# First attention of a four-layer transformer kernel: stacked rows of two batches by a selection matrix on TensorE, and the loads in another order

## The chip, the cores and the metric

One core of a Trainium2 chip runs the whole program in one launch. The metric is the device time of that launch in microseconds (us). The kernel before took 1108.44 us (median of three runs).

## What is computed

The reference is four layers, each `x = x + attention(layernorm(x))` and `x = x + ffn(layernorm(x))`, with another attention and another feed-forward block in each layer. Only the first attention is changed. For `x` and `ctx` of shape (8, 128, 512) and a mask of shape (8, 1, 512), it works on 32 patches of 128 columns (4 of each of 8 batches):

```python
q = einsum('ed,bdw->bew', Wq, x_patch) + bq        # 64 rows = 8 heads x 8
k = einsum('ed,bdw->bew', Wk, x_patch) + bk
val = einsum('ed,bdw->bew', Wv, ctx_patch) + bv
scores = einsum('bhdi,bhdj->bhij', qh, kh) / sqrt(8)
scores = where(mask > 0, scores, -1e9)
o = einsum('bhij,bhdj->bhdi', softmax(scores), vh)
out = (einsum('de,bew->bdw', Wo, gelu(o)) + bo) * mask
```

## The kernel before

The first attention is the function `l0_attention` (line 284). Each engine has its own program, written out by hand; the engines meet only at semaphores, and each runs its instructions strictly in the order written. The layers stand one behind the other with a barrier between them (`end_layer`, line 70), so the stage ends for all engines at once.

**Batches and units.** The eight batches `b` are worked through in order. A batch is two units `u` (`A0_GROUPS`, four heads each), a unit is two steps `s` (two heads each). For a batch, VectorE (DVE) takes the statistics of `x[b]` (line 100 and 102), GpSimd (POOL) makes 1/sigma of them (lines 106 and 109), DVE (b < 3) or POOL (b >= 3) normalises (lines 597, 496), and TensorE (PE) projects queries and keys together (`project`, line 694). DVE adds the bias and multiplies by `kept`, which DVE (b = 0) or POOL makes of the loaded mask (lines 608, 360). The result `qk` is split into an fp32r upper part (ScalarE, ACT, line 541) and a rest (line 653 on DVE for b = 0, line 484 on POOL for the others).

**The stacked rows.** A score matmul needs, at the partitions of its head, 26 rows: the 8 rows of the upper part twice, the rest once, a row for the maximum and a row for the mask. The kernel before gets them through DRAM: `store(b)` (lines 409 to 418) writes the parts in five DMAs to `a0_parts`, and `fetch(b)` (lines 420 to 428) reads them back in four DMAs into the stack `st`, in the order wanted. The constant rows of all batches are written once (lines 437 to 441).

**The loop over the units.** Scores (line 723), their maximum on DVE (line 628), the maximum turned on PE (line 732), added to the queries on DVE (`lower`, line 638), scores again with that subtracted (`keyed`, line 742), exponent on ACT (line 557), values (line 753), a copy and a turn (lines 564, 760), and a division on DVE. In iteration u, PE runs:

```python
turn_max(u); scores(2u+2); keyed(2u-1)
project(batch_at(u))         # u odd: batch (u + 5) // 2, so 3 at u=1, 4 at u=3 ... 7 at u=9
project_values(...)          # u even
values(u-1); scores(2u+3); keyed(2u); turn_outputs(u-1)
```

DVE runs `divide(u-2)`, `maximum(2u+2)`, `statistics(statistics_at(u))`, `keys_queries(batch_at(u))`, `lower(u)`, `maximum(2u+3)`. `statistics_at(u)` (line 383) gives batch u // 2 + 4 at even u, and batch 3 stands ahead of the loop (line 662). POOL runs, for each batch from 3 on, `first.scale(b)` (waits for the statistics), `keep_rows(b)` (waits for the mask's load), `normalise(b)`, `lower_part(b)`, lines 525 to 529.

**The queue of SyncE (SP)**, which issues all loads and stores of the stage, is in a fixed order (lines 430 to 470), with waits between; what stands behind a wait is issued after it. Here the mask of batch 3 is loaded (line 453) ahead of `store(2)` and behind `fetch(1)`.

## Time and profile before

| | |
|---|---|
| runs | 1108.44 us median, 1107.95 to 1110.77 (3 runs) |
| the profiled execution | 1100.67 us, its span 1098.9 us |
| mean granted clock of TensorE in it | 0.926 |
| busy, share of the span | PE 86%, DVE 62%, ACT 41%, POOL 34% |
| first attention | 0 to 165.6 us of the span |
| first score matmul | 28.35 us |
| first turn of a maximum (unit 0) | 34.52 us |
| DMAs up to 130 us | 21.83 MB, mean 168 GB/s |

The span is the profiled execution alone, seen from the first to the last instruction; 1.8 us of its time lie around it. In the views, L694 is line 694 of the kernel before. SPq marks the issue of a DMA, not its transfer. A TensorE row with x2 or x8 is a run of that many instructions, with the time from the first start to the last end; an fp32 matmul shows as two instructions.

### The profile page before, as it was taken

Reading aid. Unit: us, or ns where it says so; the run is one execution under the profiler, and the core shown is the slowest. Engines: PE = TensorE matmul, PEld = TensorE weight load, DVE = VectorE, ACT = ScalarE, POOL = GpSimd, SP = SyncE. Lnnn points to the kernel's source line nnn. Section 1 sums busy time; section 2 is a strip of 40 time slices with the busy share of each in tenths; the row PEclk is TensorE's granted clock in tenths of the full one; section 3 lists DMA queues with packets and bytes.
Section 4 is the critical chain, followed back from the end, with each engine's and each line's share of the span. In section 5 each row is a group of like instructions: output and inputs, shape, how many; then the busy total and the mean of one; then the engine's idle time right before and its main releaser. Section 6 shows DMA issues by size and latency. Waiting matters only on the chain. (4 is left out here: it accounts for less than half of the span.)

```text
span 1098.9 us, 14895 instructions
## 1 busy us (share of the span) xinstructions
PE 941.0 (86%) x4891; PEld 610.1 (56%) x4891; DVE 683.1 (62%) x1143; ACT 447.4 (41%) x656; POOL 374.4 (34%) x362
## 2 busy tenths in 40 slices
PE   2788786989999899999877598899986689679997
PEld 0566623756666566663445344455473455457886
DVE  2566464686687687764858753566644887445334
ACT  0255413325656566652234422344403555235130
POOL 5552021224566565651222220211220222048431
PEclk9999855999999999999889699799988999879999
DMA  6766103146977967556304100000003100032001
GB/s 158 230 169 175 63 0 140 39 164 243 342 266 269 372 202 267 201 177 216 115 23 160 39 0 1 20 1 1 1 0 153 49 0 1 5 92 77 29 10 38
DMA packets 41237, 124.00 MB, mean 113 GB/s; under 512 B 5313, under 2 KB 5761, under 8 KB 38473
## 3 DMA queue, kind: packets, MB, share of 16 engines
q1 hardware_dynamic: 33640, 98.41, 26.7%
q0 software_dynamic: 7520, 24.65, 6.8%
q8 instruction: 40, 0.66, 0.3%
q14 instruction: 37, 0.30, 0.1%
HBM read 137.19 MB, written 23.59 MB: 146 GB/s over the span
## 5 line engine op out<-in xcount | busy, mean ns | idle before, releaser
L1275 POOL DMA_INDIRECT f_picks<-f_turn_xn,f_target x47 | 106.7, 2271 | 78.9 <-ACT f_turn_xn L1164 78.0
L1691 PE MATMUL banks<-f_t_dn,f_z 128*128 128x512 f32 x188 | 88.5, 593 | 0.6 <-issue 0.6
L1419 DVE TENSOR_TENSOR f_gu_lo<-f_t_gu,f_gu_hi 128x2048 fp32r<-128x2048 f32 x24 | 55.1, 2296 | 18.1 <-ACT f_gu_hi L1150 15.2
L1269 POOL DMA_INDIRECT f_turn_xn<-f_xn_rows,f_token x47 | 48.5, 1033 | 46.0 <-DVE f_token L1413 18.7
L1419 DVE TENSOR_TENSOR f_xn_lo<-f_t_gu,f_xn_hi 128x2048 fp32r<-128x2048 f32 x23 | 52.8, 2297 | 17.5 <-ACT f_xn_hi L1150 17.5
L628 DVE TENSOR_REDUCE a_mx<-banks 128x8 f32<-128x1024 f32 x32 | 39.2, 1226 | 27.1 <-PE banks L723 27.1
L2389 ACT ACTIVATE a_e<-banks 128x1024 f32<-128x1024 f32 x32 | 32.8, 1025 | 54.1 <-PE banks L2481 54.1
L2419 DVE TENSOR_REDUCE a_mx<-banks 128x8 f32<-128x1024 f32 x32 | 39.1, 1223 | 21.8 <-PE banks L2461 21.8
L1150 ACT CAST f_gu_hi<-f_t_gu 128x2048 fp32r x24 | 45.7, 1904 | 13.4 <-DMA f_t_gu<-in_f_gu 11.2
L1150 ACT CAST f_xn_hi<-f_t_gu 128x2048 fp32r x23 | 43.8, 1903 | 13.3 <-DMA f_t_gu<-in_f_gu 9.9
L1157 ACT ACTIVATE f_sil<-banks 128x256 f32<-128x256 f32 x47 | 18.1, 384 | 75.9 <-PE banks L255 75.9
L164 PE MATMUL banks<-ident,f_turn_xn 128*128 128x128 f32 x96 | 21.7, 382 | 31.4 <-DVE f_turn_xn L172 31.4
L100 DVE BATCH_NORM_STATS2 stat<-x_res 128x6 f32<-128x512 f32 x64 | 44.4, 693 | 3.5 <-DMA x_res<-in_x 1.6
L557 ACT ACTIVATE a_e<-banks 128x1024 f32<-128x1024 f32 x32 | 32.8, 1024 | 30.3 <-PE banks L742 29.9
L1691 PEld LDWEIGHTS banks<-f_t_dn,f_z 128*128 128x128 f32 x188 | 32.1, 190 | 23.3 <-issue 23.2
L253 PE MATMUL banks<-f_gu_hi,f_xn_hi 128*128 128x512 f32 x96 | 40.0, 416 | 2.1 <-issue 2.1
L106 POOL TENSOR_TENSOR f_ahead_var_eps<-mean_var,eps 128x1 f32<-128x1 f32 x24 | 9.0, 376 | 91.6 <-DVE mean_var L102 91.6
L253 PE MATMUL banks<-f_xn_hi 128*128 128x512 f32 x92 | 38.0, 413 | 1.3 <-issue 1.3
L3154 DVE TENSOR_TENSOR f_square<-f_relu 128x512 f32<-128x512 f32 x16 | 19.5, 1224 | 30.9 <-ACT f_relu L3097 25.9
L255 PE MATMUL banks<-f_gu_hi,f_xn_lo 128*128 128x512 f32 x96 | 38.0, 396 | 0.0
L254 PE MATMUL banks<-f_gu_lo,f_xn_hi 128*128 128x512 f32 x96 | 38.0, 396 | 0.0
L164 PEld LDWEIGHTS banks<-ident,f_turn_xn 128*128 128x128 f32 x96 | 15.4, 193 | 39.7 <-DVE f_turn_xn L172 39.4
(414 smaller groups left out, 2567.6 us busy)
## 6 DMA issues: line engine op xcount, KB each, us to landing
f_t_gu<-in_f_gu SPq DMA_DIRECT2D x47, 1024.0 KB
f_t_dn<-in_f_dn SPq DMA_DIRECT2D x47, 512.0 KB
f_t_gu<-f_picks SPq DMA_DIRECT2D x8, 1024.0 KB, 5.2
a_st<-a_parts SPq DMA_DIRECT2D x32, 208.0 KB
f_xn_rows<-f_turn_xn SPq DMA_DIRECT2D x9, 256.0 KB, 2.1
x_res<-in_x SPq DMA_DIRECT2D x8, 256.0 KB, 5.6
a_out_mask<-in_mask SPq DMA_DIRECT2D x8, 256.0 KB, 6.1
a_parts<-a_qk_hi SPq DMA_DIRECT2D x8, 256.0 KB
```

Of the source, the lines that this page charges most:

```text
L100: dve.bn_stats(self.stat[:, b, :], src).then_inc(self.stat_ready, 1)
L164: mm = pe.transpose(self.core.psum[:, self.first_bank + b % 2, c * P:(c + 1) * P], self.xn[:, b % self.rows, c * P:(c + 1) * P], self.core ...
L253: pe.matmul(out, w_hi, m_hi, start=start, stop=False)
L254: pe.matmul(out, w_hi, m_lo, start=False, stop=False)
L255: return pe.matmul(out, w_lo, m_hi, start=False, stop=stop)
L628: dve.tensor_reduce(mx[:, :, PAIR * (s % 2) + A0_MAX_ROW:PAIR * (s % 2 + 1):A0_SLOT].rearrange("p w r -> p r w"), ps[:, S_BANK:S_BANK + 2, ...
L1150: act.copy(t_gu_hi[t % 2], t_gu[:, bass.ds(i, 1), :, :].rearrange("p i c n -> p (i c n)"))\
L1269: pool.indirect_dma_start(t_rows[:, t % F0_BUFS, :], None, dram["f0_xn_rows"], bass.IndirectOffsetOnAxis(ap=token[:, t:t + 1], axis=0))\
L1275: pool.indirect_dma_start(dram["f0_picks_flat"], bass.IndirectOffsetOnAxis(ap=target[:, t:t + 1], axis=0), t_y[:, t % F0_BUFS, :], None).t ...
L1419: dve.tensor_tensor(t_gu_lo[t % 2], t_gu[:, bass.ds(i, 1), :, :].rearrange("p i c n -> p (i c n)"), t_gu_hi[t % 2].bitcast(F32), ALU.subtr ...
L1691: mm = pe.matmul(ps[:, TY_BANK + t % 2, :], t_zt[:, t % 2, c, :], t_dn[:, t % F0_BUFS, c, :], start=c == 0, stop=c == F0_IC - 1)
L2419: dve.tensor_reduce(mx[:, tiles, A2_MAX_ROW:P:A2_SLOT].rearrange("p m r -> p r m"), ps[:, S_BANK:S_BANK + 2, :].rearrange("p r (m j) -> p ...
```

## The change

Of batches 0 and 1 (`A0_DIRECT = 2`) the rows no longer go through DRAM. A selection matrix is drawn on chip out of the identity: VectorE clears a scratch of 128x1024, ScalarE copies four patterns of the identity into it and casts it to fp32r (128x1024), and a second small block of constant rows is made in the same way. For each of units 0 to 3, `stack(u)` on TensorE then makes the 128 rows of queries and the 128 rows of keys in PSUM: three matmuls with one row of contraction for the constant rows, and four with the selection matrix, two of the upper part and two of the rest. ScalarE copies the queries out of PSUM into the stack (`keep_queries`), VectorE the keys (`keep_keys`). Units 0 and 1 are stacked ahead of the loop, 2 and 3 at the end of iteration 0; behind them, in iteration 0, now stand the projection of batch 2 and the values of batch 0, which stood ahead of the loop. The clearing of the stack on POOL goes. Batches 2 to 7 are stored and fetched as before. The order of the loads, of POOL's early work and of the statistics is another: `statistics_at(u)` gives batch u // 2 + 3 at even u > 0, with batch 3 at the end of iteration 0.

The diff, cut (scratch names and semaphores left out):

```diff
+            sel = st[:, A0_DIRECT, 0:2, :]
+            drawn, drawn_rows = e[:, 0, 0:2, :], e[0:1, 0, 2:4, :]
+            off_rows = qm[0:1, 0:A0_DIRECT, :]
...
+            def sel_bank(u, keys):
+                return ((6, 7), (2, 1), (2, 1), (0, 2))[u][keys]
...
             def statistics_at(u):
-                return u // 2 + A0_EARLY + 1 if u % 2 == 0 and u // 2 + A0_EARLY + 1 < B else None
+                return u // 2 + A0_EARLY if u % 2 == 0 and 0 < u and u // 2 + A0_EARLY < B else None
...
                     load_x(0)
                     sp.dma_start(core.raw[:, 0, 0:A0_FIRST[-1]], dram["a0_first"]).then_inc(first_loaded, 16)
+                    load_mask(0)
+                    sp.dma_start(mask_rows, dram["mask"][0:A0_DIRECT].unsqueeze(0)).then_inc(mask_rows_loaded, 16)
+                    load_x(1)
+                    load_mask(1)
+                    load_x(2)
                     sp.dma_start(off_row[:, :], dram["mask"]).then_inc(mask_row_loaded, 16)
-                    load_mask(0)
-                    load_x(1)
-                    load_x(2)
...
-                    store(0)
-                    sp.wait_ge(fixed_stored, 16 * 3)
-                    load_mask(1)
                     load_mask(2)
                     load_ctx(0)
-                    fetch(0)
                     load_x(3)
-                    store(1)
+                    sp.wait_ge(fixed_ready, 2)
...
+                    sp.wait_ge(fixed_stored, 16 * 3)
+                    load_ctx(1)
                     load_x(4)
-                    load_ctx(1)
-                    fetch(1)
+                    store(2)
                     load_mask(3)
-                    store(2)
                     load_x(5)
                     load_ctx(2)
                     fetch(2)
...
(POOL)
-                    clear(0)
+                    pool.memset(mx[:, :, :], 0.0).then_inc(mx_zeroed, 1)
+                    for i in range(2):
+                        pool.memset(fixed[:, i, :], float(i)).then_inc(fixed_ready, 1)
                     first.scale(pool, 0)
+                    for i in range(2):
+                        pool.memset(v[:, i, :, :, :], 0.0).then_inc(zeroed, 1)
+                    first.scale(pool, 1)
...
                     keep_rows(1)
-                    lower_part(1)
-                    clear(1)
-                    keep_rows(2)
-                    lower_part(2)
+                    first.scale(pool, 2)
...
+                    lower_part(1)
+                    keep_rows(2)
+                    lower_part(2)
...
(ACT)
+                    def keep_queries(u):
+                        act.wait_ge(sel_done, 2 * u + 1)
+                        act.copy(q_of(u, slice(0, P), slice(0, D)), ps[:, sel_bank(u, 0), :]).then_inc(st_q_ready, 1)
-                    for b in range(A0_EARLY):
-                        upper_part(b)
-                    take_values(0)
+                    upper_part(0)
+                    keep_queries(0)
+                    keep_queries(1)
+                    upper_part(1)
                     for u in range(UNITS + 1):
...
+                        if u == 0:
+                            keep_queries(2)
+                            keep_queries(3)
+                            upper_part(2)
+                            take_values(0)
...
(DVE)
+                    def keep_keys(u):
+                        dve.wait_ge(sel_done, 2 * u + 2)
+                        dve.tensor_copy(k_of(u, slice(0, P), slice(0, D)), ps[:, sel_bank(u, 1), :])\
+                           .then_inc(st_k_ready, 1)
...
                     normalise(1)
-                    keys_queries(1)
-                    normalise(2)
-                    keys_queries(2)
+                    keep_keys(0)
+                    keep_keys(1)
+                    statistics(2)
                     dve.wait_ge(mx_zeroed, 1)
                     maximum(0)
+                    keys_queries(1)
                     maximum(1)
-                    statistics(A0_EARLY)
+                    normalise(2)
...
+                        if u == 0:
+                            keep_keys(2)
+                            keep_keys(3)
+                            keys_queries(2)
+                            statistics(A0_EARLY)
...
(PE)
+                    def stack(u):
...
+                        pe.matmul(queries, row_of(A0_MASK_ROW), ones_row, start=True, stop=False)
+                        pe.matmul(keys, row_of(A0_MAX_ROW), ones_row, start=True, stop=False)
+                        pe.matmul(keys, row_of(A0_MASK_ROW), off_rows[:, b, :], start=False, stop=False)
+                        pe.wait_ge(qk_hi_ready, b + 1)
+                        pe.matmul(queries, sel[:, 0, jobs[0]], hi, start=False, stop=False)
+                        pe.matmul(keys, sel[:, 0, jobs[1]], hi, start=False, stop=False)
+                        pe.wait_ge(qk_lo_ready, b + 1)
+                        pe.matmul(queries, sel[:, 1, jobs[0]], lo, start=False, stop=True).then_inc(sel_done, 1)
+                        pe.matmul(keys, sel[:, 1, jobs[1]], lo, start=False, stop=True).then_inc(sel_done, 1)
...
-                    for b in range(A0_EARLY):
-                        project(b)
-                    project_values(0)
-                    pe.wait_ge(const_ready, 4)
+                    project(0)
+                    stack(0)
+                    stack(1)
+                    project(1)
                     scores(0)
                     scores(1)
...
+                        if u == 0:
+                            stack(2)
+                            stack(3)
+                            pe.wait_ge(st_q_ready, 2 * A0_GROUPS)
+                            pe.wait_ge(st_k_ready, 2 * A0_GROUPS)
+                            project(2)
+                            project_values(0)
```

`stack(3)` waits ahead of its first matmul for the queries of unit 2 to be copied out of bank 2 (`st_q_ready` 3).

## Rows read from the trace of the kernel before

**Rows 1.** timeline 0 to 29 us: start, us, engine, line, operation, idle before it

```profile
6.38 2.04 PE L694 MATMUL banks<-a_xn,raw 128*128 128x512 f32 x2 [6.38 <-DVE a_xn L597]
...
16.84 1.41 SPq L399 DMA_DIRECT2D a_out_mask<-in_mask  x2
...
21.37 2.01 POOL L360 TENSOR_SCALAR a_kept<-a_out_mask,a_cols 128x512 f32<-128x512 f32 x1 [9.11 <-DMA a_out_mask<-in_mask]
...
23.49 0.75 DVE L608 SCALAR_TENSOR_TENSOR a_qk<-banks,a_cols,a_kept 128x512 f32<-128x512 f32 x1 [11.63 <-POOL a_kept L360]
...
27.37 0.57 SPq L418 DMA_DIRECT2D a_parts<-a_qk_lo  x1
...
28.35 1.11 PE L723 MATMUL banks<-a_st 26*128 26x128 f32 x8
```

**Rows 2.** timeline 34 to 45 us, all engines

```profile
34.52 1.11 PE L732 MATMUL banks<-ident,a_mx 128*128 128x128 f32 x4 [1.32 <-DVE a_mx L628]
...
34.72 0.37 SPq L399 DMA_DIRECT2D a_out_mask<-in_mask  x1
...
39.40 1.11 PE L742 MATMUL banks<-a_qm,a_st 26*128 26x128 f32 x8 [0.19 <-DVE a_qm L638]
...
40.55 2.00 POOL L360 TENSOR_SCALAR a_kept<-a_out_mask,a_cols 128x512 f32<-128x512 f32 x1 [3.18 <-DMA a_out_mask<-in_mask]
...
42.54 2.09 POOL L496 TENSOR_SCALAR a_xn<-x_res,mean_var,rstd 128x512 f32<-128x512 f32 x1
...
44.68 2.08 PE L694 MATMUL banks<-a_xn,raw 128*128 128x512 f32 x2 [1.85 <-POOL a_xn L496]
```

**Rows 3.** timeline 52 to 94 us, projections of batches 4 to 7, statistics before them

```profile
53.42 0.18 DVE L102 BATCH_NORM_AGGREGATE mean_var<-stat 128x2 f32<-128x6 f32 x1
...
58.39 2.07 PE L694 MATMUL banks<-a_xn,raw 128*128 128x512 f32 x2 [1.39 <-POOL a_xn L496]
...
61.96 0.33 PE L723 MATMUL banks<-a_st 26*128 26x128 f32 x2
...
67.10 0.18 DVE L102 BATCH_NORM_AGGREGATE mean_var<-stat 128x2 f32<-128x6 f32 x1
...
70.60 1.13 PE L694 MATMUL banks<-a_xn,raw 128*128 128x512 f32 x2
...
72.87 0.55 PE L723 MATMUL banks<-a_st 26*128 26x128 f32 x6
...
81.51 1.13 PE L694 MATMUL banks<-a_xn,raw 128*128 128x512 f32 x2
...
93.15 1.12 PE L694 MATMUL banks<-a_xn,raw 128*128 128x512 f32 x2 [0.66 <-POOL a_xn L496]
```

**Rows 4.** timeline of TensorE at 186 us, a dense stretch of fp32r matmuls

```profile
186.65 0.63 PE L254 MATMUL banks<-f_xn_lo,f_gate_hi 128*16 128x512 f32 x1
...
187.08 0.63 PE L255 MATMUL banks<-f_xn_hi,f_gate_lo 128*16 128x512 f32 x1
...
188.38 0.39 PE L253 MATMUL banks<-f_xn_hi,f_gate_hi 128*16 128x512 f32 x1
...
188.60 0.40 PE L254 MATMUL banks<-f_xn_lo,f_gate_hi 128*16 128x512 f32 x1
```

**Rows 5.** groups by line and form, VectorE, whole span

```profile
L2148 DVE CAST a_q_st<-banks 128x512 fp32r<-128x512 f32 x16 | 11.0, 687 | 7.4 <-PE banks L2251 7.4
```

**Rows 6.** DMA issues up to 130 us: size, us from issue to landing

```profile
raw<-in_a_first SPq DMA_DIRECT2D x1, 98.0 KB, 2.5
```

**Rows 7.** timeline at 10 us: 1/sigma of batch 1 on POOL

```profile
10.11 0.19 POOL L106 TENSOR_TENSOR in_ahead_var_eps<-mean_var,eps 128x1 f32<-128x1 f32 x1 [0.72 <-DVE mean_var L102]
...
10.38 0.57 POOL L109 TENSOR_TENSOR rstd<-in_ahead_var_eps,neg_half 128x1 f32<-128x1 f32 x1
```

**Rows 8.** windows: stretch, length, busy us of PE, PEld, DVE, ACT, POOL, clock, DMA share, GB/s

```profile
58.00:60.00 2.00, 1.61 (x2) 0.50 (x2) 0.24 (x1) 0.13 (x1) 0.33 (x1) 0.54 0.84 209
...
116.00:118.00 2.00, 1.99 (x36) 1.60 (x40) 0.67 (x2) 0.13 (x1) 0.00 (x0) 0.55 0.00 0
```

99 lines of the change are left out of this document (72 added, 27 removed).

## The prediction

> **What bounds the kernel now.** I read the page for the shares, then the timeline of the first 60 us, the waits in it, the timelines of VectorE, POOL, TensorE and of SP's queue up to 165 us, and the windows for the clock. The stage of the change ends in a barrier, so what its end gains or loses goes to the total whole. The start is bound by the way through DRAM: batch 0 is projected at 6.38, and its first score matmul comes at 28.35 [rows 1]. Between them lie the store, the fetch, and the mask of batch 1, which is issued behind the store at 16.84 and releases POOL only at 21.37. The first maximum is turned at 34.52 [rows 2]. From there the units run at their own pace, and something else binds: PE works in order, and in every odd unit stands a projection of a later batch ahead of the work of the unit. In unit 1 PE waits for POOL's normalised batch 3 until 44.68, after POOL has waited for the mask of that batch (issued 34.72, used 40.55) [rows 2]. In unit 3 it waits again (1.39 us, project at 58.39). In units 5 and 7 (70.60 and 81.51) it waits for nothing, in unit 9 for 0.66 us [rows 3]. So the question is not how early unit 0 starts, but when batch 3 can be projected, and whether batches 4 to 7 are ready when PE gets there.
>
> **The early start.** Removed are store(0), store(1), fetch(0), fetch(1) and three clears of the stack, added are 28 matmuls, eight copies out of PSUM and the drawing of the matrix. The drawing ends well ahead of the first use at about 10 us: it is a clear and a few copies while x is loaded, and where it ran over, PE would wait for it by that much; I put it at nothing, with 1 us as the upper end. project(0) ends at 8.4. The 14 matmuls of stacks 0 and 1 are fp32r with 512 columns. The trace has such a stream at both levels of the clock: 0.43 us from start to start at 1.2 GHz (186.65 to 187.08), 0.22 at 2.4 GHz (188.38 to 188.60), with the granted clock at one half and at one [rows 4]. At the start PE is at the lower level by its durations (2.04 for a projection [rows 1] against 1.13 at 70.60 [rows 3]). So 14 x 0.43 = 6.0 and 0.2 for the wait for the parts: 14.6, then project(1) to 16.7, and the scores of step 0 there. Up to keyed(0) follow one behind the other four scores and the turn, 1.11 each [rows 2], and three maxima of 1.2: 9.2, so keyed(0) at about 25.9 against 39.40 [rows 2]. A dense stretch of 6 us stands ahead of this, though, and in the trace such a stretch brought the clock up [rows 4]. At the upper level for part of the way (stack 1, project(1) and the scores of step 0) keyed(0) is at 23.7, and at the upper level all the way at about 22. I take 23.7, which lies between. The lead over before is then 15.7 us.
>
> **Where the lead goes.** keyed(0) ends at 24.8. Stack 2 and stack 3 come then, and stack 3 waits for the copy of unit 2's queries: 7 x 0.43 = 3.0, 0.3 for the end of the last matmul and 0.69 for a copy [rows 5]; stack 3 can start behind the copy of the queries, one matmul ahead of the stack's end, at 28.2. Its keys are copied at 32.2 by the same sum, and at 30.6 with the clock at its upper level by then; I take 31.5. Only then may project(2) write its bank: 1.13 to 2.04, so 32.7. Before, from qk in VectorE to the end of the last issue of its store took 23.49 to 27.94, 4.45 us [rows 1]. SP comes to the mask of batch 3 only behind `store(2)`: 37.2, where it was issued at 34.72 before. The order of these two is turned round, and that is the step that costs. **The load** of this mask is priced by the mask of batch 1, which stood behind a store too: 16.84 to 21.37, 4.5 us. Its ends are 2.5 us (a load of 98 KB with little ahead of it [rows 6]) and 5.8 us (34.72 to 40.55, with a fetch ahead). 4.5 is the nearest, as its queue is the same. So POOL begins at 41.7, and needs 2.00 for kept and 2.09 for the normalised batch (40.55 to 44.68: 4.1): **project(3) at 45.9 against 44.68, 1.2 us later than before.** All the lead is spent in PE's wait in unit 1. With PE at the lower level all the way, keyed(0) is at 25.9, project(2) ends at 36.2 and project(3) starts at 49.3: 4.6 later. At the upper level all the way from stack 1, project(2) ends at 28.3, and project(3) starts at 41.4: 3.3 earlier.
>
> The Trainium skill (DMA: Bandwidth & Descriptors, Anatomy of one DMA — SWDGE (gpsimd) path) has a fit of 2.0 us and the bytes over 436e3 per us, which makes 2.6 us for this mask's 256 KB instead of 4.5, and by it the sum below would be 1.9 less, 1115.1. The trace speaks against it for a mask behind a store.
>
> **The statistics.** They slip by one even unit. Batch 4's now stand in unit 2, batch 5's in 4, batch 6's in 6, batch 7's in 8, where before the batch after it stood. POOL works in order: 1/sigma (10.11 to 10.95, with a tenth ahead of it: 0.93 [rows 7]), kept 2.00, normalise 2.09, together 5.05 from the end of the statistics to the projection. Nothing hides this any more, as both the statistics and the use stand two units nearer.
> - Batch 4: statistics end at 53.60 + 5.05 = 58.65 against 58.39 [rows 3]: +0.3.
> - Batch 5: 67.28 + 5.05 = 72.35 against 70.60: +1.75.
> - Batch 6: the same, one period of 10.91 later (70.60 to 81.51): +1.75.
> - Batch 7: 67.28 + 21.82 + 5.05 = 94.15 against 93.15: +1.0.
>
> Together +4.8, each on top of the shift so far, since the statistics move with the unit.
>
> **The clock.** Before project(4) PE stood for 1.39 us, and the granted clock was 0.54 in the window behind it; in the window from 116 it was 0.55, behind a stretch of short waits with no projection [rows 8]. From such a projection to the next scores it took 3.57 (58.39 to 61.96) against 2.27 at the upper level (70.60 to 72.87) [rows 3]: 1.3 us for a fall. PE now stands 1.75 us at batches 5 and 6 and 1.66 at batch 7, longer than at batch 4, but at batch 7 with 0.66 before it did not fall. I take two falls of three, 2.6 us; the ends are 0 and 3.9.
>
> **At nothing**: the removed clears on POOL, whose idle time hides them; the traffic of two batches less through DRAM, as neither PE nor DVE waits for a fetch in any of the rows from 52 us on; the copies of stacks 2 and 3 on ACT and VectorE, which are in the sum already, and what lies in unit 1 between, which PE's wait for batch 3 covers. If that cover is gone (project(3) early), they count as in the sum of project(3).
>
> **Sum**: +1.2 +4.8 +2.6 = +8.6 us in this stage. Against the profiled execution (1098.9 span, 1100.67 with what lies around it) that is 1109.3; the median of the runs is 7.8 above the profiled one, and I add the same to it: 1108.4 + 8.6 = **1117.0 us**.
>
> **The rivals.**
> - *The clock stays up.* Stacks 0 and 1 bring PE to 2.4 GHz and it stays there. For it: a dense stretch of this kind rose to it in the trace. Against: in units 0 and 1 PE mostly waits for maxima, and before it was at the lower level there for all of 28 to 45 us. Then project(3) is 3.3 earlier, PE comes to batches 5 to 7 without a fall, and the fall at 58 may go too: -3.3 +4.8 -1.3 = +0.2, 1108.6, not slower. It decides from the point at which project(3) starts before 40 us. Chance 0.14.
> - *The clock stays down up to unit 1.* +4.6 +4.8 +3.9 = +13.3, 1121.7. Chance 0.18.
> - *No fall at batches 5 to 7.* +1.2 +4.8 = +6.0, 1114.4. Chance 0.20.
> - *The lead is kept*: the change does what it says for the total, since neither mask 3 nor the statistics hold PE. Unit 0 turned some 15 us earlier would give 1093. For it: SP may have less queued, and the mask land early. Against: the order of SP, PE and POOL is written out, and a mask issued at 37 can't feed a projection before 43. Chance 0.06.
>
> **The numbers.** The forecast as summed has 0.42. A measurement of this kernel can tell about 0.3%, 3.3 us, from no change. Slower by more: the forecast, the low clock, and most of the case without falls, with 0.02 to 0.03 off for its lower end: 0.75. Faster: the kept lead and a little of the first rival: 0.08. Within: 0.17. The range takes in the first rival's 1108.6 and the second's 1121.7: 1108.5 to 1122.
>
> **What would show it.** Scores of step 0 at 15 to 17 us, keyed(0) at 23 to 26. SP's issue of mask 3 at 36 to 41, behind the last piece of store(2). PE idle for 7 us or more ahead of project(3), released by POOL, at 44 to 49. The projections of batches 5 to 7 released by POOL with 1.6 us or more of idle time, where two of them had none, and project(7) at 95 to 102 against 93.15. Stage end at 170 to 178 against 165.6. The forecast is wrong if project(3) comes before 42, or if the idle time ahead of project(5) and project(6) is under 1 us; and it is wrong in its clock term if the granted clock stays at one behind them.

## The result, and the profile after

The changed kernel takes 1126.1 us (median of 4 runs, 1124.74 to 1128.23) against 1108.2 for the kernel before (4 runs, 1106.48 to 1110.77): a ratio of 1.0161, 95% interval 1.0135 to 1.0188. It is 17.9 us slower, where 8.6 were forecast; the direction was right, the size was not, and the time lies above the range. The profiled execution took 1128.23 us, with a span of 1126.4. One execution of the first experiment below (1127.89 us) fell in a slower state of the chip, at a lower granted clock, and is left out of its numbers.

The start of the changed kernel, from the timelines of VectorE and TensorE (start, duration, engine, line, tiles; in brackets the idle time ahead and what ended it; `...` marks rows left out):

```profile
5.39 2.04 DVE L636 TENSOR_SCALAR a_xn<-x_res,mean_var,rstd 128x512 f32<-128x512 f32 x1 [0.95 <-POOL rstd L109]
7.58 2.05 PE L750 MATMUL banks<-a_xn,raw 128*128 128x512 f32 x2 [7.58 <-DVE a_xn L636]
...
15.73 0.63 PE L799 MATMUL banks<-a_qk_lo,a_st 128*128 128x512 f32 x1
16.16 0.63 PE L800 MATMUL banks<-a_qk_lo,a_st 128*128 128x512 f32 x1
...
18.42 1.11 PE L813 MATMUL banks<-a_st 26*128 26x128 f32 x8
...
23.55 1.09 PE L822 MATMUL banks<-ident,a_mx 128*128 128x128 f32 x4 [1.41 <-DVE a_mx L667]
...
36.82 2.04 PE L750 MATMUL banks<-a_xn,raw 128*128 128x512 f32 x2 [0.83 <-ACT a_st L597]
```

The early start is there: the first scores come at 18.42 instead of 28.35 [rows 1], the first maximum is turned at 23.55 instead of 34.52 [rows 2]. But the stacks' matmuls are still 0.43 us apart at the end of stack 1 (15.73, 16.16), the distance of 1.2 GHz [rows 4], and the scores behind them take 1.11 for eight, as at the start of before. The signs that the forecast gave for this part are missed: 15 to 17 us for the first scores, and 23 to 26 for keyed(0), which starts at 27.60. Project(2) runs from 36.82 to 38.9, where 32.7 was forecast for its end.

The same view from project(2) to project(3), with SP's queue:

```profile
38.91 0.75 DVE L647 SCALAR_TENSOR_TENSOR a_qk<-banks,a_cols,a_kept 128x512 f32<-128x512 f32 x1 [2.18 <-PE banks L750]
...
42.93 0.57 SPq L433 DMA_DIRECT2D a_parts<-a_qk_lo  x1
43.55 0.46 SPq L414 DMA_DIRECT2D a_out_mask<-in_mask  x1
...
48.29 2.00 POOL L371 TENSOR_SCALAR a_kept<-a_out_mask,a_cols 128x512 f32<-128x512 f32 x1 [5.83 <-DMA a_out_mask<-in_mask]
...
52.41 2.08 PE L750 MATMUL banks<-a_xn,raw 128*128 128x512 f32 x2 [10.02 <-POOL a_xn L507]
```

This is the chain of the forecast link by link: the store's last piece, the mask behind it, POOL's two operations (the second from 50.27 to 52.35), and PE idle for 10.02 us. Only its start is late: mask 3 is issued at 43.55, where 36 to 41 was given, and project(3) starts at 52.41, outside 44 to 49.

TensorE's timeline of the later units: the projections of batches 4 to 7, most of the turns of the maxima (one a unit), the first output projection (L867), and on VectorE the first operation of the next stage:

```profile
58.72 1.12 PE L822 MATMUL banks<-ident,a_mx 128*128 128x128 f32 x4 [0.25 <-DVE a_mx L667]
67.04 1.12 PE L822 MATMUL banks<-ident,a_mx 128*128 128x128 f32 x4 [0.26 <-DVE a_mx L667]
69.16 2.07 PE L750 MATMUL banks<-a_xn,raw 128*128 128x512 f32 x2
74.57 0.66 PE L822 MATMUL banks<-ident,a_mx 128*128 128x128 f32 x4 [0.54 <-DVE a_mx L667]
80.02 0.66 PE L822 MATMUL banks<-ident,a_mx 128*128 128x128 f32 x4 [0.23 <-DVE a_mx L667]
82.94 2.08 PE L750 MATMUL banks<-a_xn,raw 128*128 128x512 f32 x2 [1.65 <-POOL a_xn L507]
...
89.25 1.11 PE L822 MATMUL banks<-ident,a_mx 128*128 128x128 f32 x4 [0.25 <-DVE a_mx L667]
...
99.68 2.07 PE L750 MATMUL banks<-a_xn,raw 128*128 128x512 f32 x2
...
105.19 0.66 PE L822 MATMUL banks<-ident,a_mx 128*128 128x128 f32 x4 [0.54 <-DVE a_mx L667]
...
113.56 2.08 PE L750 MATMUL banks<-a_xn,raw 128*128 128x512 f32 x2 [1.64 <-POOL a_xn L507]
...
173.91 1.38 PE L867 MATMUL banks<-a_gelu,a_wo 64*128 64x512 f32 x2
...
196.34 1.00 DVE L172 TENSOR_SCALAR f_turn_xn<-x_res,mean_var,rstd 128x512 f32<-128x512 f32 x2 [2.35 <-PEq L75]
```

Two kinds of unit can be seen. With turns of 0.66 us a unit takes 5.45 us (74.57 to 80.02), half of the 10.91 between two projections before [rows 3]; with turns of 1.12 it takes 8.3 us (58.72 to 67.04). PE is hardly idle in either. The projections start later than before by 7.7, 10.8, 12.3, 18.2 and 20.4 us, and the stage ends 30.7 later (196.34 against 165.63). PE waits for POOL at batches 5 and 7 (1.65 and 1.64, forecast 1.75 and 1.66), and not at all at batches 4 and 6, where 1.7 and 1.75 were forecast. The window from 60 to 120 us shows what PE did in the rest (busy time of PE, its loads, VectorE, ScalarE and POOL; then the granted clock, the share of the DMA engines, GB/s). First before, then after:

```profile
60.00:120.00 60.00, 51.13 (x819) 38.74 (x818) 41.09 (x60) 31.67 (x41) 19.48 (x16) 0.96 0.57 149
```
```profile
60.00:120.00 60.00, 53.71 (x613) 38.34 (x614) 33.84 (x51) 24.93 (x32) 24.39 (x20) 0.77 0.56 139
```

PE is busier than before and gets through 613 matmuls where it did 819. (The column of the clock says 1.00 up to the first change that the trace records, in after at 82 us; by the durations PE was low there up to some 72 us, so the 0.77 is still too high.)

From project(3) to project(7) it takes 61.2 us (52.41 to 113.56) instead of 48.5 (44.68 to 93.15), though the waits for POOL in it grow only from 2.05 to 3.29. The eight units between them at 5.45 make 43.6 in both. What is left is 2.8 before and 14.3 after. The turns tell how it is made up, before in these rows:

```profile
50.27 0.66 PE L732 MATMUL banks<-ident,a_mx 128*128 128x128 f32 x4 [0.54 <-DVE a_mx L628]
...
63.95 0.66 PE L732 MATMUL banks<-ident,a_mx 128*128 128x128 f32 x4 [0.54 <-DVE a_mx L628]
...
85.76 0.65 PE L732 MATMUL banks<-ident,a_mx 128*128 128x128 f32 x4 [0.38 <-DVE a_mx L628]
```

In both kernels PE comes out of some of its waits at the lower level. Before, this happens at batches 3 and 4, and both times it is up again at the next turn (0.66 at 50.27 and 63.95), at some 1.3 us each. After, it happens at batches 3 and 5, and both times it stays low over two turns and comes up only behind the next projection, ahead of which PE did not wait (69.16 and 99.68). From the projection to the third turn behind it such a spell takes 22.2 us (52.41 to 74.57, 82.94 to 105.19), where the same stretch at the upper level took 15.2 before (70.60 [rows 3] to 85.76): 7 us a spell, and two of them are the 14.3. So to come low out of a wait has two prices, 1.3 us or 7.

Behind project(7), with no wait for POOL left, PE is low again for most of the way: at the first output projection, 173.91 against 138.52 in the row of before that follows, the shift is 35.4 us instead of 20.4, which is 15 us more, as much as some five units at the lower level.

```profile
138.52 2.07 PE L777 MATMUL banks<-a_gelu,a_wo 64*128 64x512 f32 x2
```

From there to the end of the stage (196.34 against 165.63, 30.7 later) 4.7 us come back, since now it is before that is at the lower clock (2.07 for this operation, where after has 1.12 and 1.09 from its second batch on).

Of the 30.7 us, project(3) makes 7.7, the waits for POOL at the later batches 1.2, and the rest, 21.8 (11.5 + 15.0 - 4.7), goes by the units to the clock. In the stages behind, another 3.2 us come back (the spans differ by 27.5).

The profiled execution of before lies 7.5 under the median given here, that of after 2.1 over its own. So this pair differs by 27.6 us, the medians by 17.9: the two traces show the mechanism somewhat larger than it is on the whole.

### The profile page after: what moved, and what is told of

The parts are those of the page before. It is cut to its first block and busy times, and to the rows that moved or that the text cites. A ratio compares the mean times of both kernels' runs of the same rounds, so it can differ in the third digit from the quotient of the medians.

```text
span 1126.4 us, 14951 instructions
## 1 busy us (share of the span) xinstructions
PE 972.3 (86%) x4916; PEld 636.7 (57%) x4919; DVE 689.2 (61%) x1151; ACT 453.3 (40%) x666; POOL 375.7 (33%) x360
## 5 line engine op out<-in xcount | busy, mean ns | idle before, releaser
L1373 POOL DMA_INDIRECT f_picks<-f_turn_xn,f_target x47 | 114.6, 2439 | 73.8 <-ACT f_turn_xn L1262 73.4
L667 DVE TENSOR_REDUCE a_mx<-banks 128x8 f32<-128x1024 f32 x32 | 39.2, 1226 | 49.3 <-PE banks L813 49.3
L1517 DVE TENSOR_TENSOR f_gu_lo<-f_t_gu,f_gu_hi 128x2048 fp32r<-128x2048 f32 x24 | 55.1, 2294 | 15.8 <-ACT f_gu_hi L1248 13.9
L2517 DVE TENSOR_REDUCE a_mx<-banks 128x8 f32<-128x1024 f32 x32 | 39.1, 1223 | 21.8 <-PE banks L2559 21.8
```

What stands on the lines that cost most here:

```text
L667: dve.tensor_reduce(mx[:, :, PAIR * (s % 2) + A0_MAX_ROW:PAIR * (s % 2 + 1):A0_SLOT].rearrange("p w r -> p r w"), ps[:, S_BANK:S_BANK + 2, ...
L1373: pool.indirect_dma_start(dram["f0_picks_flat"], bass.IndirectOffsetOnAxis(ap=target[:, t:t + 1], axis=0), t_y[:, t % F0_BUFS, :], None).t ...
L1517: dve.tensor_tensor(t_gu_lo[t % 2], t_gu[:, bass.ds(i, 1), :, :].rearrange("p i c n -> p (i c n)"), t_gu_hi[t % 2].bitcast(F32), ALU.subtr ...
L2517: dve.tensor_reduce(mx[:, tiles, A2_MAX_ROW:P:A2_SLOT].rearrange("p m r -> p r m"), ps[:, S_BANK:S_BANK + 2, :].rearrange("p r (m j) -> p ...
```

## The experiments

The expectations name two theories. **W**: the waits for POOL, made longer by the later statistics and by the order of `store(2)` and mask 3, cost their own length, and the clock falls because of them, so that taking a wait away gives both back. **C**: the lower clock is entered and left by itself, whatever the wait, so that taking a wait away gives back its length alone. Each label below is one kernel; its ratio is to the kernel before on the same chip, with the 95% interval. Executions of all these kernels scatter more than the first runs had shown (25 of the kernel before gave 1100.47 to 1116.73 around 1107.75), so small differences are taken from ratios with intervals.

### The statistics back in their old place

```diff
-                return u // 2 + A0_EARLY if u % 2 == 0 and 0 < u and u // 2 + A0_EARLY < B else None
+                return u // 2 + A0_EARLY + 1 if u % 2 == 0 and 0 < u and u // 2 + A0_EARLY + 1 < B else None
...
                             statistics(A0_EARLY)
+                            statistics(A0_EARLY + 1)
```

> The changed kernel with the statistics back at their old even units (batches 3 and 4 at the end of iteration 0, 5 in unit 2, 6 in unit 4, 7 in unit 6); all else as changed. Changed kernel 1126.1 us. Theory W (the slipped statistics make PE wait for POOL ahead of the projections of batches 5 and 7, 1.65 and 1.64 us in the changed trace, and the clock falls because of these waits): both waits go, and with them the low clock behind them (82 to 102 us and 113 to 160 us), 3.3 us for the waits and 12 to 17 for the clock: 1106 to 1111 us. Theory C (TensorE's low clock is entered and left by itself, whatever the wait): only the waits go, about 1123 us.

Measured: 1110.8 us (9 runs, 1106.41 to 1119.89), ratio 1.0025 (0.9985 to 1.0065). That is 15.3 under the changed kernel (14.6 if the execution left out is counted), from a part for which the forecast had 4.8 in waits and 2.6 in clock. It is what W expected, and 12 us under what C did: much more comes back than the length of the waits. The profiled execution is the one left out, so nothing is rested on its trace.

### The mask ahead of the store

```diff
                     load_x(4)
-                    store(2)
                     load_mask(3)
+                    store(2)
```

> The changed kernel with the load of mask 3 issued ahead of store(2), one line moved. If the place of this load holds the projection of batch 3 (52.41 us in the changed trace), POOL starts on kept at 42.5, and project(3) at about 46.6, 5.8 us earlier: 1120 us. If what follows is set by the clock and not by the wait, the 5.8 us come back or are lost by other low stretches: anything from 1116 to 1126. If the load was no cause, 1126.

Measured: 1121.5 us (4 runs), ratio 1.0139 (1.0066 to 1.0213), 4.6 under the changed kernel. TensorE's timeline:

```profile
45.84 2.08 PE L750 MATMUL banks<-a_xn,raw 128*128 128x512 f32 x2 [4.18 <-POOL a_xn L507]
...
75.77 1.12 PE L750 MATMUL banks<-a_xn,raw 128*128 128x512 f32 x2 [1.63 <-POOL a_xn L507]
```

The start of project(3) and the time are as expected (46.6 and 1120 us). Project(3) is 6.6 us earlier than after (45.84 against 52.41), so the order of these two spent most of the lead, and from there on each projection stays ahead of its time in after. Project(5) runs at the upper level here (1.12) in spite of a wait of 1.63 us. For the total the step between medians, 4.6 us, points the same way, but the two intervals (1.0066 to 1.0213 and 1.0135 to 1.0188) lie over each other, so that its size is not secured.

### Both

```diff
-                return u // 2 + A0_EARLY if u % 2 == 0 and 0 < u and u // 2 + A0_EARLY < B else None
+                return u // 2 + A0_EARLY + 1 if u % 2 == 0 and 0 < u and u // 2 + A0_EARLY + 1 < B else None
...
                     load_x(4)
-                    store(2)
                     load_mask(3)
+                    store(2)
```

> Both of the former edits together. Theory W: the sum, 1100 to 1105 us, faster than the kernel before (1108.2). Theory C: 5.8 + 3.3 less than changed, about 1117 us.

Measured: 1108.8 us (10 runs, 1102.84 to 1114.51), ratio 0.9996 (0.9959 to 1.0033), between the two expectations: 8 under C's and 4 over the upper end of W's. With both edits undone what is left of the change (the selection matrix and the rest of the new order) alters nothing that can be measured. In its trace project(3) comes at 45.32, and PE then waits 2.84 us for POOL ahead of project(4), since POOL waits 5.41 us for mask 4: the next mask holds the lead up in turn. Against the second experiment the statistics are worth 12.7 us, and this step is secured; against the first one the mask is worth 2.0, within the intervals of both.

### The waits kept, the clock held up

The changed kernel with matmuls whose result nobody reads, put where PE waits: 24 ahead of project(3), 8 ahead of each later projection, 4 ahead of the values in units with no projection of either kind. They have 128 rows and 512 columns in fp32r and write a bank that the next operation overwrites. No wait is taken away, and fills stand also where PE did not wait (batches 4 and 6).

```diff
+                    def fill(bank, n):
+                        for _ in range(n):
+                            pe.matmul(ps[:, bank, :], warm[:, 0:P], warm[:, :], start=True, stop=True)
...
                     def project(b):
-                        pe.wait_ge(xn_ready, b + 1)
                         if b >= 1:
                             pe.wait_ge(qk_ready, b)
...
+                        if b >= A0_EARLY:
+                            fill(QK_BANK, 24 if b == A0_EARLY else 8)
+                        pe.wait_ge(xn_ready, b + 1)
...
+                        if batch_at(u + 1) is None and values_at(u + 1) is None:
+                            fill(V_BANK, 4)
```

> The changed kernel with idle time of TensorE filled: ahead of the wait for the normalised batch stand 24 (batch 3) or 8 (batches 4 to 7) fp32r matmuls 128x512 of constant data into the bank that the projection then overwrites, and 4 ahead of the values in units without projection. They compute nothing that is used. No wait is removed. Theory C or W with the clock as the larger part: TensorE stays at 2.4 GHz from the projection of batch 3 on, a unit takes 5.5 us instead of 8.3, and the time falls by 15 to 20 us to 1106 to 1111. If the waits for POOL and the mask are what costs, nothing or a few us more: 1126 to 1132.

Measured: 1105.1 us (10 runs, 1100.21 to 1113.55), ratio 0.9971 (0.9929 to 1.0012): 21 us under the changed kernel, with more work on PE and the same order of loads and statistics. Its window and project(3):

```profile
60.00:120.00 60.00, 55.81 (x788) 42.88 (x778) 39.78 (x61) 29.04 (x38) 24.37 (x20) 1.00 0.64 157
```
```profile
51.63 1.13 PE L761 MATMUL banks<-a_xn,raw 128*128 128x512 f32 x2 [2.29 <-POOL a_xn L509]
```

Project(3) is nearly as late as after (51.63 against 52.41), and the granted clock is 1.00 instead of 0.77, with 0.65 or 0.66 us for every turn in the window; the time is just under the expected 1106 to 1111. So holding the clock up gives back as much as the change lost, with its order of loads and statistics still there. This shows what the clock costs in this kernel. It does not decide between C and a W with the clock as its larger part (the expectation gives both the same time), and it does not show that the whole loss of the change was clock, since the kernel before may gain by fills as well.

### The same two edits in the kernel before

The kernel before, with its statistics one even unit later, where the change puts them:

```diff
-                return u // 2 + A0_EARLY + 1 if u % 2 == 0 and u // 2 + A0_EARLY + 1 < B else None
+                return u // 2 + A0_EARLY if u % 2 == 0 and 0 < u and u // 2 + A0_EARLY < B else None
```

> The kernel BEFORE the change with one line of the change: the statistics one even unit later (batch 4 in unit 2 up to batch 7 in unit 8). The sum of the prediction for this part: +4.8 us of waits and +2.6 for the clock, 1115 us against 1107.8. Theory W with a low clock that lasts, as in the runs with the changed kernel (1126.1 to 1111.5 when it is taken back, 14.6 us): 1120 to 1123 us. If the statistics count only behind a late batch 3: 1108 to 1110.

Measured: 1118.7 us (10 runs, 1112.39 to 1123.44), ratio 1.0082 (1.0044 to 1.0121), 10.8 us more. Project(4), the second turn behind it, and the window:

```profile
58.73 2.08 PE L694 MATMUL banks<-a_xn,raw 128*128 128x512 f32 x2 [1.64 <-POOL a_xn L496]
...
73.36 1.12 PE L732 MATMUL banks<-ident,a_mx 128*128 128x128 f32 x4 [0.26 <-DVE a_mx L628]
```
```profile
60.00:120.00 60.00, 53.71 (x623) 38.68 (x626) 33.67 (x51) 24.91 (x32) 19.54 (x16) 0.67 0.56 144
```

Project(3) comes as before (44.90), project(4) waits 1.64 instead of 1.39, and from there the clock is 0.67 instead of 0.96: PE stays low over both turns behind project(4) (1.12 at 73.36), and in the same way behind project(6), which waits 1.64 too. At batches 5 and 7, to which PE comes late, it waits for nothing. That speaks for W again: one line that lengthens waits brings the low spells. The statistics' +7.4 of the forecast (4.8 and 2.6) are 10.8 here; the interval reaches from 4.9 to 13.4, so that this run alone does not say that the price was too low. It lies between the two expectations, 1115 and 1120 to 1123.

The kernel before with fills, built like those above:

```diff
+                        if b >= A0_EARLY:
+                            fill(QK_BANK, 6 if b == A0_EARLY else 6)
...
+                        if batch_at(u + 1) is None and values_at(u + 1) is None:
+                            fill(V_BANK, 4)
```

> The kernel BEFORE the change with the filling matmuls (6 ahead of each projection from batch 3 on, 4 ahead of the values in units without projection). If the low stretches of the kernel before (58 to 62, 116 to 120, 130 to 160 us in its trace) are worth something, 3 to 8 us less: 1100 to 1104 us, and less spread between executions. If its clock is no loss, the six fills of 1.3 us each ahead of the projections that don't wait show: 1110 to 1115.

Measured: 1093.8 us (4 runs, 1089.35 to 1099.96), ratio 0.9873 (0.9787 to 0.9959), 14.2 under before, more than the 3 to 8 expected. So the kernel before pays for the lower clock too. Its project(3), and the window:

```profile
45.84 1.91 PE L705 MATMUL banks<-a_xn,raw 128*128 128x512 f32 x2
```
```profile
60.00:120.00 60.00, 54.88 (x798) 41.88 (x800) 39.65 (x59) 29.96 (x39) 19.44 (x16) 0.97 0.56 147
```

This is the pair to set side by side. With the clock up in both (1.00 and 0.97), the changed kernel takes 11.3 us more (1105.1 and 1093.8; ratios 0.9971 and 0.9873, whose intervals overlap by 0.003), and its stage ends 6.4 us later in the traces (167.67 and 161.26), as project(3) stands 5.8 later (51.63 and 45.84). The number of fills differs somewhat (8 and 6 ahead of each later projection). So a part of the loss, 6 to 11 of the 17.9 us by these numbers, stays when the clock is up; the traces put it to the late batch 3.

### Does a stack bring the clock up?

The forecast let the 14 matmuls of stacks 0 and 1 bring PE up, as a dense fp32r stretch had done in the trace [rows 4]. Three of the seven matmuls of a stack have one row of contraction. The probe puts four dense series ahead of the first projection of the kernel before, all of fp32r matmuls with 512 columns: 32 with one row, 32 with the identity as stationary operand (128 rows, nearly all zeros), 32 with 128 full rows, 48 with one row. Only its first 53 us are read; its total (1147.8 us, one run) says nothing more.

```diff
+                    for _ in range(32):
+                        pe.matmul(ps[:, E_BANK, :], warm[0:1, 0:P], warm[0:1, :], start=True, stop=True)
+                    for _ in range(32):
+                        pe.matmul(ps[:, E_BANK, :], pick[:, :], warm[:, :], start=True, stop=True)
+                    for _ in range(32):
+                        pe.matmul(ps[:, E_BANK, :], warm[:, 0:P], warm[:, :], start=True, stop=True)
+                    for _ in range(48):
+                        pe.matmul(ps[:, E_BANK, :], warm[0:1, 0:P], warm[0:1, :], start=True, stop=True)
```

> Not a version but a probe: the kernel BEFORE, with four dense series of fp32r matmuls with 512 moving columns ahead of its first projection: 32 with one row of contraction (1x128 by 1x512), 32 with the identity as stationary (one element per column that is not zero, like the selection matrix), 32 with full constant data (128x128 by 128x512), 48 with one row again. Spacing tells the level of the clock: 0.43 us low, 0.22 to 0.23 high. Theory R (rows count: a matmul with one row of contraction keeps no clock up): series 1 low throughout, series 2 and 3 rise, series 4 falls back. Theory Z (zeros count): series 1 and 2 low, series 3 rises. Theory D (only density counts, and the stacks were too broken up): series 1 rises within some 5 us, and all the rest is high.

TensorE's timeline of the probe, and its windows (PE busy, granted clock):

```profile
5.01 13.99 PE L790 MATMUL banks<-a_warm 1*128 1x512 f32 x32 [5.01 <-ACT a_pick L542]
18.93 9.50 PE L792 MATMUL banks<-a_warm,a_pick 128*128 128x512 f32 x32
28.26 7.42 PE L794 MATMUL banks<-a_warm 128*128 128x512 f32 x32
35.61 16.92 PE L796 MATMUL banks<-a_warm 1*128 1x512 f32 x48
```
```profile
22.00:23.00 1.00, 1.00 (x4) 1.00 0.00 0
23.00:24.00 1.00, 1.00 (x6) 1.00 0.00 0
...
40.00:41.00 1.00, 1.00 (x5) 0.59 0.00 0
41.00:42.00 1.00, 1.00 (x4) 0.50 0.00 0
```

The first series takes 13.9 us for 32 matmuls, 0.435 each: 1.2 GHz from end to end, without a gap. In the second the rate rises at 23 (six started in a window of 1 us instead of four), the third takes 0.23 each, and in the fourth, one row again, the clock falls at 40 although PE never stops. This is the theory R of the expectation in all four series. One-row matmuls neither raise the clock here nor keep it; a stationary operand that is nearly all zeros, but 128 rows deep, does raise it. (Up to 40 us the column of the granted clock is again without a recorded change; there the durations have to be read.)

Then the changed kernel with the constant rows widened from one to 128 partitions, zeros in the rest, so that all seven matmuls of a stack have 128 rows:

```diff
-            const_rows = st[0:1, A0_DIRECT, 2:4, :]
-            drawn, drawn_rows = e[:, 0, 0:2, :], e[0:1, 0, 2:4, :]
+            const_rows = st[:, A0_DIRECT, 2:4, :]
+            drawn, drawn_rows = e[:, 0, 0:2, :], e[:, 0, 2:4, :]
...
-                        pe.matmul(keys, row_of(A0_MASK_ROW), off_rows[:, b, :], start=False, stop=False)
+                        pe.matmul(keys, row_of(A0_MASK_ROW), off_all[:, b, :], start=False, stop=False)
```

> The changed kernel with nothing but the blocks of constant rows widened from one partition to 128, with zeros in the others (the results are the same, and each matmul takes the same 512 columns; POOL clears 128x1024 once more at the start). Six of the fourteen matmuls of stacks 0 and 1 then no longer have a single row of contraction. Theory R: TensorE rises to 2.4 GHz within stacks 0 and 1 or behind them, the stacks 2 and 3 run at the upper level at least in part, project(3) comes at 46 to 50 us instead of 52.4, and the time is 1115 to 1122 against 1126.1. If the rows of these six matmuls don't matter: project(3) at 52.4, 1126 us, within its spread.

```profile
12.07 0.63 PE L802 MATMUL banks<-a_qk_lo,a_st 128*128 128x512 f32 x1
12.50 0.57 PE L803 MATMUL banks<-a_qk_lo,a_st 128*128 128x512 f32 x1
12.91 0.39 PE L795 MATMUL banks<-a_st 128*128 128x512 f32 x1
13.13 0.39 PE L796 MATMUL banks<-a_st 128*128 128x512 f32 x1
...
14.53 1.02 PE L753 MATMUL banks<-a_xn,raw 128*128 128x512 f32 x2
...
31.80 1.10 PE L753 MATMUL banks<-a_xn,raw 128*128 128x512 f32 x2 [0.83 <-ACT a_st L599]
...
46.49 2.07 PE L753 MATMUL banks<-a_xn,raw 128*128 128x512 f32 x2 [11.70 <-POOL a_xn L508]
```

Now the clock rises between the two stacks (0.43 to 0.22 us apart), project(1) takes 1.02 instead of 1.91, project(2) ends at 32.9, where the forecast had 32.7, and project(3) starts at 46.49, where it had 45.9. This is what was expected if the rows count. Measured: 1120.4 us (6 runs, 1116.5 to 1123.38), ratio 1.0123 (1.0075 to 1.0171), 5.7 under the changed kernel by the medians, with intervals that overlap. The gaps differ a little, too: between the two stacks there are 0.41 us from start to start (12.50 to 12.91) instead of 0.56 (12.58 to 13.14), in the middle of the first stack 0.84 instead of 0.55, so in this kernel rows and gaps are not wholly parted; the probe, without any gap, parts them.

The same trace shows the two prices of a fall side by side, behind project(5) and project(6):

```profile
74.73 2.08 PE L753 MATMUL banks<-a_xn,raw 128*128 128x512 f32 x2 [1.65 <-POOL a_xn L508]
...
80.19 0.66 PE L825 MATMUL banks<-ident,a_mx 128*128 128x128 f32 x4 [0.54 <-DVE a_mx L669]
...
88.56 2.08 PE L753 MATMUL banks<-a_xn,raw 128*128 128x512 f32 x2 [1.65 <-POOL a_xn L508]
...
94.86 1.11 PE L825 MATMUL banks<-ident,a_mx 128*128 128x128 f32 x4 [0.25 <-DVE a_mx L669]
```

The wait is the same 1.65 us and both projections are low. Behind the first PE is up at the next turn; behind the second it is low over two turns and up at the third, at 110.83. What decides between them was not found. It may be one reason why executions of the same kernel scatter as they do; no run shows that.

### All together, and the kernel before with the same help

First the changed kernel with the statistics and the mask early and fewer fills:

```diff
+                            fill(QK_BANK, {3: 10, 4: 6}.get(b, 0))
...
+                            fill(V_BANK, 4)
```

> The changed kernel with the early statistics, the early mask load and fills (10 ahead of projection 3, 6 ahead of projection 4, 4 ahead of the values in units without projection). Waits gone and clock up from batch 3 on: project(3) at 45 as with the two edits alone, then 5.5 us a unit: 12 to 15 us less than those edits alone in their traced run from 60 us on, 1094 to 1099 us, faster than both kernels. If the fills only move the low stretches elsewhere: 1105 to 1110.

Then the same with fills in unit 0, too:

```diff
+                    fill(E_BANK, 8)
                     project(0)
...
                     scores(0)
+                    fill(E_BANK, 5)
                     scores(1)
+                    fill(E_BANK, 5)
...
+                        if u == 0:
+                            fill(E_BANK, 5)
```

> The same with 8 fills ahead of project(0) and three times 5 in the waits of unit 0. If they bring the clock up before 20 us, the stacks take 1.6 us instead of 3.0 and project(3) comes at 38 to 41 instead of 45: 4 to 7 us less than without them, 1088 to 1094 us. If the dense part at the start is too short for it, the fills cost their own time: 1 to 3 us more than without them.

The same with 14 more around stacks 2 and 3:

```diff
+                            fill(M_BANK, 8)
                             stack(2)
+                            fill(M_BANK, 3)
                             stack(3)
+                            fill(M_BANK, 3)
```

> The run with all edits and the early fills (1092.05 us), with 8 more fills ahead of stack(2), 3 ahead of stack(3) and 3 ahead of project(2). In the trace without them the clock was low from 25 to 38 us, through both stacks. If the fills keep it up there, project(3) comes 3 to 4 us earlier (36 instead of 39.9), 1088 to 1089 us. If stacks make it fall all the same, the fills cost 1 to 3 us: 1093 to 1095.

And the kernel before with the fills of unit 0, a long one ahead of project(2), and those ahead of projections 5 to 7 left out again:

```diff
+                            fill(QK_BANK, {3: 6, 4: 6}.get(b, 0))
...
+                        if b == 2:
+                            fill(E_BANK, 32)
                         project(b)
```

> The kernel BEFORE (rows of all batches through DRAM) with the fills, also ahead of project(0), 32 ahead of project(2) and three times 5 in unit 0, where TensorE is idle. It tells what the selection matrix is worth once the clock is up. If the early start counts: project(3) stays at about 42 to 45, set by the load of mask 3, and the time is 3 to 6 us above the run before in this list, 1091 to 1094. If the way through DRAM costs nothing more: the same as that run.

| kernel | median us (runs, range) | ratio (95%) | stage end, its trace |
|---|---|---|---|
| all three | 1096.7 (4, 1089.66 to 1102.36) | 0.9893 (0.9801 to 0.9986) | 163.9 |
| and fills in unit 0 | 1092.1 (4, 1086.99 to 1097.05) | 0.9854 (0.9768 to 0.9939) | 153.9 |
| and around stacks 2, 3 | 1096.8 (6, 1089.05 to 1101.53) | 0.9865 (0.9813 to 0.9916) | 166.4 |
| before, with fills | 1093.8 (4) | 0.9873 (0.9787 to 0.9959) | 161.3 |
| before, more fills | 1093.9 (6, 1091.89 to 1100.89) | 0.9867 (0.982 to 0.9914) | 160.6 |

The first, second and last came within their expectations (1094 to 1099, 1088 to 1094, 1091 to 1094), the third did not (1088 to 1089, or 1093 to 1095). The second has the lowest median, 34 us under the changed kernel and 16 under the one before, but the intervals of all five overlap. Its project(3):

```profile
39.86 1.12 PE L762 MATMUL banks<-a_xn,raw 128*128 128x512 f32 x2
```

Project(3) at 39.86 is 4.8 us earlier than before, and in its trace the stage ends 6.7 us earlier than in that of before with more fills. Between the medians of the two nothing can be told: the intervals 0.9768 to 0.9939 and 0.982 to 0.9914 lie over each other. What the selection matrix is worth once everything else is put right stays open between nothing and some 7 us. Why the fills around stacks 2 and 3 brought nothing was not tested, but the trace of that kernel shows how its time went:

```profile
42.09 2.08 PE L762 MATMUL banks<-a_xn,raw 128*128 128x512 f32 x2 [3.33 <-POOL a_xn L509]
```

The ten fills ahead of project(3) run at the upper level here and are over in 2.56 us instead of 4.30, so that they no longer cover the wait for POOL. PE stands for 3.33 us, comes out low, and stays low over the next two turns (1.12 us at 48.40 and 56.72).

## Why the prediction was wrong in size and right in direction

**What bounds the kernel: right.** The lead (9.9 us at the first scores, 11.0 at the first turn, 11.8 at keyed(0) where 15.7 were forecast) ends in PE's wait in unit 1, released by POOL behind mask 3, which is queued behind the last piece of `store(2)`. Moving the mask ahead brings project(3) 6.6 us forward.

**The step "a dense stretch of 6 us stands ahead of this, though, and in the trace such a stretch brought the clock up": failed.** The stretch was there and the clock did not rise. The row it was taken from is a stream of matmuls 128 rows deep [rows 4]; three of a stack's seven have one row, and the probe shows that such matmuls do not raise the clock and let it fall. Project(2) ended at 38.9 instead of 32.7, and these 6.2 us are nearly all of the 6.5 by which project(3) was late (52.41 against 45.9). So the term of +1.2 us for project(3) measured +7.7. The rival "the clock stays down up to unit 1" had 36.2 and 49.3 for these two. Of its remaining 2.7, 1.2 come from VectorE's first normalisation, 2.04 us beside a clear on POOL. With 128 rows in all seven the forecast's own times came out within 0.6 us, by some luck, since project(0) started 1.1 us later there than the sum has it (7.51). A slip in the sum itself is small: its terms put the start of stack 3 at 28.4, not 28.2.

**The links behind it: right.** From qk(2) to the issue of mask 3 4.64 us (forecast 4.5), from there to its use 4.74 (4.5), POOL 4.1 (4.1). So the price of a mask behind a store held, against the 2.6 us that the prediction worked out from the Trainium skill's fit (which is for DMAs that GpSimd issues; SP issues this one).

**The statistics: the mechanism right, its sum of waits too high.** 1.65 and 1.64 us at batches 5 and 7 (1.75 and 1.66). At batches 4 and 6 PE waits for nothing, because it came there late by itself: the slower PE covered the wait. Together PE's waits for POOL at batches 4 to 7 grew by 1.2 us and not by 4.8. The forecast had named idle time under 1 us ahead of project(5) and project(6) as a sign that it is wrong; at project(6) it came.

**The step "1.3 us for a fall", two falls of three: failed, and it is the larger one.** The prediction priced a fall by one projection and what stood behind it up to the next scores, which is a case where the clock came back within the unit. In the trace of after it did not: each of the two low spells between project(3) and project(7) went on up to the next projection and cost 7 us, and behind project(7) the low units cost some 15 more, 4.7 of which came back. The term of 2.6 us measured 21.8 in this pair of traces. PE is busy nearly all the time in these spells. The fills show that the time lies in the clock: -21 us in the changed kernel, with no wait removed. As the kernel before gains 14.2 by fills, the clock's share of the 17.9 us by the medians is smaller than in the traces, 7 to 12 us, and still well over 2.6. That longer waits bring the clock down is shown by the statistics in either kernel (-15.3 and +10.8, against 7.4 in the forecast), of which only the first is clear of 7.4 by its intervals. What lets the clock come back at once in one case and not in the other stays open.

**The rivals.** That no falls come (0.20), that the clock stays up (0.14) and that the lead is kept (0.06) did not come. The case that came is the low clock up to unit 1 (0.18, 1121.7), with the falls behind it dearer than in any case that the range took in. The direction was no luck, as it rests on the wait in unit 1. In the size two errors go against each other: 4.8 us of waits that came to 1.2, and a clock term far too small.

The Trainium skill (TensorE: Matmul & The Clock Gate, Part 1) calls the cost of the low clock at the start less than 1% of a typical kernel's span. Here the clock is low again and again up to 170 us, and the fills regained 14.2 us of 1108 in the kernel before, 1.3%, and 21 in the changed kernel, 1.9%. The Trainium skill also says there that activity releases the throttle; in the probe matmuls 128 rows deep did and those of one row did not.

## What to carry to other kernels

When a change moves waits on TensorE, price each wait twice: by its length, and by how many units behind it run at 1.2 instead of 2.4 GHz (here 8.3 instead of 5.45 us a unit), read from the durations of the same instruction at both levels. Give a fall its dear price, too, and not only the one that the trace before happens to show. If a stretch is to bring the clock up because one in the trace did, compare the rows (partitions) of its matmuls, too, and not only the columns: here 128 rows did and one row did not; what lies between was not tried. Where PE has to wait for another engine anyway, a few full matmuls that nobody reads can be worth more than the edit that shortens the wait, and an order of loads that puts a store ahead of what the next wait is for should be looked at first.

## What was unexpected of the hardware

- One-row fp32r matmuls of 512 columns take the same time as those of 128 rows at the same clock (0.43 us), and leave the clock where it is, or let it fall: 32 of them in 13.9 us with no rise, and a fall from 1.00 to 0.50 between 40 and 42 us in the fourth series.
- The lower level can hold for long: after ran whole units with PE busy throughout at 8.3 us each without rising, and rose behind the projections at 69.16 and 99.68, once also with no projection near (a turn of 0.66 at 144.18). What in the units' small matmuls keeps it down was not tried.
- The same wait of 1.65 us ahead of a projection cost 1.2 us of clock in one place and 7 in another of the same trace (project(5) and project(6) of the kernel with full rows).
- VectorE's first normalisation took 2.04 us at 5.39, beside POOL's clears of 128x1024 (5.30 to 7.16), where the same instruction took 0.85 before, beside a POOL operation on 8x512 (5.32 to 7.28). All nine traces with the change have the 2.04. By the Trainium skill (SBUF — State Buffer, Who interferes with whom), some VectorE operations and POOL's block each other for whole instructions; the 2.04 fits that, the 0.85 shows that not every operation of POOL's does it, and it was not tested here.
